# Gated projection weights and the residual's bias of all four batches: made by GpSimd at the start of the attention block instead of by VectorE in the block before

## The reference

```
mod = (silu(c) @ wmod).reshape(B, 6, 1, 256)       # sa, ca, ga, sb, cb, gb
ga  = sign(ga) * max(|ga|, 0.25)
h   = layernorm(x) * (1 + ca) + sa
x   = x + ga * (attention(h) @ W_O + b_O)          # 8 heads, low-rank q, k, v
h   = layernorm(x) * (1 + cb) + sb
x   = x + gb * experts(h)                          # top-1 routing, capacity 768
```

## Time and profile before

| | before |
|---|---|
| time of three runs | 975.48, 975.59, 976.31 us |
| profiled execution: its own time | 975.42 us |
| profiled execution: span | 973.7 us |
| TensorE busy | 865.9 us (89%) |
| VectorE busy | 670.3 us (69%) |
| GpSimd busy | 607.0 us (62%) |
| ScalarE busy | 563.6 us (58%) |

### The profile page before, as it was taken

The page is one execution under the profiler, slowest core; times in us unless marked ns, Lnnn a source line. Parts: engine busy times, 40 slices in busy tenths (PEclk is TensorE's granted clock), DMA queues, the critical chain, the costliest instruction groups (busy, mean ns, idle before and its releaser), DMA issues. The chain is left out here.

```text
span 973.7 us, 20139 instructions
## 1 busy us (share of the span) xinstructions
PE 865.9 (89%) x7974; PEld 605.8 (62%) x7974; DVE 670.3 (69%) x1266; ACT 563.6 (58%) x968; POOL 607.0 (62%) x438
## 2 busy tenths in 40 slices
PE   4895899999999999999999979860799999999995
PEld 1351366666666666666666758760476777677764
DVE  4767887878887878887888609843276567565743
ACT  3641476767676767676767745653447545644650
POOL 5200388888888888888888974786324533452342
PEclk9995699999999999999999989965799999999998
DMA  9911000000000000000000014378434534353110
GB/s 276 335 68 33 1 1 2 3 2 2 2 1 2 2 2 3 2 2 2 2 2 3 2 51 162 120 260 277 145 107 135 183 101 162 129 172 103 43 52 20
DMA packets 52368, 72.32 MB, mean 74 GB/s; under 512 B 11618, under 2 KB 44583, under 8 KB 52048
## 3 DMA queue, kind: packets, MB, share of 16 engines
q1 hardware_dynamic: 42322, 53.93, 16.8%
q0 software_dynamic: 7680, 16.87, 5.3%
q10 hardware_dynamic: 2272, 0.24, 0.2%
HBM read 46.76 MB, written 29.67 MB: 78 GB/s over the span
## 5 line engine op out<-in xcount | busy, mean ns | idle before, releaser
L809 POOL TENSOR_TENSOR prob_lo<-prob 128x1024 f16<-128x1024 f32 x208 | 390.4, 1896 | 120.4 <-ACT prob L781 119.9
L833 DVE TENSOR_REDUCE part_max<-x_ps 128x1 f32<-128x512 f32 x512 | 325.2, 681 | 79.0 <-PE x_ps L730 75.7
L781 ACT ACTIVATE prob<-st_ps 128x512 f32<-128x512 f32 x512 | 281.6, 595 | 114.4 <-PE st_ps L718 108.6
L730 PE MATMUL x_ps<-KX,CQ 98*128 98x512 f16 x512 | 205.0, 405 | 4.0 <-DVE KX L845 1.4
L718 PE MATMUL st_ps<-CQ,KX 99*128 99x512 f16 x512 | 197.2, 386 | 2.8 <-ACT prob L781 1.5
L1304 POOL DMA_INDIRECT out<-yo,xb x48 | 47.7, 994 | 153.4 <-DVE yo L1411 148.5
L756 PE MATMUL acc_ps<-VV,prob 128*128 128x65 f16 x1664 | 128.5, 193 | 2.9 <-POOL prob_lo L809 2.9
L756 PE MATMUL acc_ps<-VV,prob_lo 128*128 128x65 f16 x1664 | 128.1, 193 | 0.0
L756 PEld LDWEIGHTS acc_ps<-VV,prob 128*128 128x128 bf16 x1664 | 116.2, 98 | 18.0 <-DVE both L852 5.0
L756 PEld LDWEIGHTS acc_ps<-VV,prob_lo 128*128 128x128 f16 x1664 | 108.6, 97 | 21.5
L1334 ACT ACTIVATE act_f<-g_ps,cols 128x768 f32<-128x768 f32 x64 | 57.7, 901 | 104.4 <-PE g_ps L1457 103.0
(11 more groups left out here) (172 smaller groups left out, 1256.7 us busy)
## 6 DMA issues: line engine op xcount, KB each, us to landing
w1f<-in_L_ffn_w SPq DMA_DIRECT2D x8, 1024.0 KB, 5.0
w2f<-in_L_ffn_w SPq DMA_DIRECT2D x8, 1024.0 KB
xbuf<-zeros SPq DMA_DIRECT2D x7, 910.0 KB, 17.2
xb<-xbuf SPq DMA_DIRECT2D x8, 780.0 KB
x<-in_L_attn_h_t SPq DMA_DIRECT2D x8, 512.0 KB, 9.0
out<-x SPq DMA_DIRECT2D x4, 1024.0 KB
tbuf<-x SPq DMA_DIRECT2D x4, 1024.0 KB
tbuf<-gb_row SPq DMA_DIRECT2D x4, 1024.0 KB
```

The costliest lines, as they stand in the source:

```text
L730: mm(x_ps[i % 3][:], queries_of[:, n % 2, b * P:(b + 1) * P, j], KX[0:QROWS, n % KRING, f * HALF:(f + 1) * HALF], start=True, stop=True).t ...
L781: nc.scalar.activation(prob[:, k, f * HALF:(f + 1) * HALF], st_ps[i % 2][:], ACT.Exp).then_inc(exp_done, 1)
L809: nc.gpsimd.tensor_tensor(prob_lo[:, k, :], prob[:, k, :], prob_top[:, k, :], ALU.subtract).then_inc(sub_pool, 1)
L833: nc.vector.tensor_reduce(part_max[:, n % 2, j, f:f + 1], x_ps[((n * ST + j) * 2 + f) % 3][:], AX.X, ALU.max).then_inc(smax_done, 1)
```

## The change

The three instructions of `prepare` leave VectorE's list in the first block. The same three are issued by GpSimd, for b = 0 to 3 one after the other, at the head of its list in the second block, ahead of its first `subtract`. The waits for `mod_in`, `side_done` and `ln_xn` are gone with the move; the waits of the instructions on each other are kept. At the end of its second block GpSimd waits for the last of them. `gbias` moves from the memory of the first block to that which is kept through the second.

```diff
@@ memory kept through the second block
+        gbias = sb(inner, "gbias", [P, D])
         mz = sb(inner, "mz", [P, 2, ST], fp16)
@@ memory of the first block
-        gbias = sb(one, "gbias", [P, D])
@@
+        def prepare(pool, b):
+            nc.gpsimd.tensor_tensor(projb[:, b, :, :], proj[:],
+                                    mod[:, b, GA, :].unsqueeze(1).broadcast_to([P, KD, D]), ALU.mult).then_inc(scaled, 1)
+            if b:
+                pool.wait_ge(biased, b)
+            nc.gpsimd.tensor_tensor(gbias[:], attn_bias[:], mod[:, b, GA, :], ALU.mult).then_inc(gbias_done, 1)
+            pool.wait_ge(gbias_done, b + 1)
+            nc.gpsimd.tensor_tensor(x1[:, b * ST:(b + 1) * ST, :], x1[:, b * ST:(b + 1) * ST, :],
+                                    gbias[:].unsqueeze(1).broadcast_to([P, ST, D]), ALU.add).then_inc(biased, 1)
@@ first block, VectorE (the function prepare of L442 to L454 goes)
                 keys_low(2)
-                prepare(0)
                 queries_low(2)
                 side_out(FOLD)
                 side_out(FOLD + 1)
                 take_values(2)
-                prepare(1)
                 keys_low(3)
-                prepare(2)
                 queries_low(3)
                 take_values(3)
-                prepare(3)
@@ second block, GpSimd
+                for b in range(B):
+                    prepare(pool, b)
                 for p, k in slots():
@@
                 normalise(HEADS - 1)
+                pool.wait_ge(biased, B)
```

More of the change, by code:

```diff
@@ L440, in take_values @@
                                             ALU.add).then_inc(v_done, 1)
[L442 to L454, removed]
                 v.wait_ge(turned_rows, 1)
```

## The result

The changed kernel takes 971.67 us, the median of six runs (970.03 to 972.17), against 975.83 us for the kernel before in the same comparison: 4.16 us less, a ratio of 0.9955 with a 95% interval of 0.9942 to 0.9967. The forecast was 970.2 us in a range of 967.8 to 972.9, with 76% on 969.0 to 971.4: the measured median lies in the range, 0.3 us outside that narrower band. The profiled execution took 971.64 us (span 969.9), 3.78 us under that of before (975.42).

The account below looks back on a forecast made before the run. VectorE was taken to bound the kernel only at the first block's end; 2.09 and 3.26 us made 5.35, GpSimd's work cost nothing, so 975.42 - 5.35 = 970.07 us, as a median 970.2, range 967.8 to 972.9.

Parts of the forecast that it names:

- VectorE alone ends the block: End of first block: the boundary waits for VectorE only, which would end at 77.31 instead of 82.66 us, 5.35 us earlier.
- Its two terms: At the boundary: 2.09 us from `queries_low(3)` released by ScalarE instead of VectorE's queue, 3.26 us from `prepare(3)` gone.
- The other 8.3 us: First block: of 13.6 us taken off VectorE, this part lay beside the wait for TensorE and ScalarE and gains nothing.
- GpSimd's twelve instructions: Start of attention: 24.1 us plus 0.8 us of waits, ending at 102.5 us, 1.9 us ahead of the first `subtract`.
- the line through two rows: GpSimd price from below, through L809 and L816: 1.66 ns an element and 0.19 us fixed, 21.0 us for four batches.
- L816's whole ratio: GpSimd price from above: 2.41 ns an element, 6.80 us a batch, 27.2 us in all.
- Cover behind the release: Start of attention: TensorE wants the first `subtract` 3.80 us after its end, so GpSimd may end that much later without loss.
- rival 2: GpSimd as the bound at attention's start: 972.7 us in mild form (6%), 981.2 us in slow form (3%).
- No disturbance between GpSimd and VectorE: Start of attention: VectorE's maxima keep their time beside GpSimd (683 and 681 ns before); GpSimd is priced by L816.
- Everything behind the boundary moves as a whole: From attention to the kernel's end: all comes 5.35 us earlier, since the boundary alone releases attention.
- Rival 1: Start of attention: TensorE's shorter pause keeps the clock from falling, 2.4 us more gained, 967.8 us; 8%.
- Rival 3: Attention or third block: other clock phases or something unseen take the gain back, 975.6 us if all; 7% in full or mostly.

Follow-up runs that it names:

- last_only: Against the changed kernel: only batch 3's three instructions go to GpSimd, those of batches 0 to 2 stay on VectorE; 972.52 us, ratio 0.9969 to before.
- first_three: Against the changed kernel: only batches 0 to 2 go to GpSimd, batch 3 stays at the end of VectorE's list; 973.91 us, ratio 0.9982 to before.
- more_2: The changed kernel with two unneeded products of `projb`'s size added behind the twelve instructions on GpSimd; 971.85 us, ratio 0.9945 to before.
- more_6: The changed kernel with six unneeded products of `projb`'s size added behind the twelve instructions on GpSimd; 980.12 us, ratio 1.0042 to before.
- early_pool: Against the changed kernel: GpSimd does batches 0 to 2 already in its first block, only batch 3 in the second; 973.98 us, ratio 0.9984 to before.
- warm: The changed kernel with twelve tiny VectorE instructions in the old places and unneeded TensorE products in its pause and at attention's start; 966.65 us, ratio 0.9898 to before.
- warm_before: The kernel before, twelve instructions still on VectorE, with unneeded TensorE products in its pause (34) and at attention's start; 972.91 us, ratio 0.9972.

## Why the prediction was right, step by step

- **VectorE alone ends the block; 5.35 us at the boundary.** Right. Measured 5.18, with `keys_low(2)` already 0.18 us later than before (59.28 to 59.46), ahead of every instruction of the change: 5.36 us of its own. Its two terms were measured apart: 3.26 as 3.26 and 2.09 as 2.10 us, counted from `keys_low(2)`.
- **The other 8.3 us, beside the wait for TensorE and ScalarE, are worth nothing.** Right: 8.0 us of idle time appear in front of the three `low` steps, and `last_only` and `first_three` give at the boundary what the list says.
- **GpSimd's twelve instructions: 21.0 to 27.2 us, 24.1 taken, and 0.8 us for waits.** The size was off, not the mechanism. `projb` took 1.26, `gbias` 0.72, x1 4.50 us, and from 77.79 to 103.84 it is 26.05 us with the waits, against 24.9. The four x1 additions have a median of 4506 ns, between the 3.60 us that the line through two rows gave and the 4.9 us of L816's whole ratio. The forecast margin of 1.9 us ahead of the first `subtract` shrank to 0.39.
- **Cover behind the release, 3.8 us more.** Right in kind: `more_2` makes the `subtract` 2.0 us late and loses nothing. In the changed kernel the cover is 3.3 us (the first `subtract` ends at 106.13, the first L748 starts at 109.47). The price beyond it, given in rival 2 as one for one, was too low by more than half: `more_6` loses 8.4 us when the first L748 comes 3.9 us later.
- **No disturbance between GpSimd and VectorE.** Right at this place: VectorE's maxima keep 683 ns (22 of them between 84 and 100 us) beside GpSimd's additions. No row of before showed that it is VectorE's reading of PSUM that keeps the two apart; that was the author's estimate. One block earlier the step would have been wrong: in `early_pool` a cast from SBUF to SBUF took 2.89 instead of 0.37 us, while a TENSOR_SCALAR that reads PSUM kept its 0.57 us.
- **Everything behind the boundary moves as a whole.** This is the step that did not hold, and the median lies 1.4 us above the forecast. In the profiled pair the start of attention gained 0.83 us, attention lost 0.83 again (0.72 of it in two new pauses), the third block's first quarter took 0.83 and what follows 0.57. Only the pauses are tied to the change by an experiment. The start of attention and the first quarter go with the clock's moments, which the forecast carried as ±1.2 us.
- **Rival 1, the clock does not fall.** It fell as the forecast had it, within 77 to 78 us (granted 0.60 in that window, 0.50 behind it). The price of 2.4 us was too low: the profiles show 3.0 us in `warm` and 3.4 in `warm_before`.
- **Rival 3, given back.** It was put down as all or nothing. Between a fifth and a third of the 5.35 us went (4.16 were left between the medians, 3.78 in the profiled pair), in part by what this rival named, a longer stretch at granted 0.50 in the third block (4.8 instead of 3.1 us).
- **The range.** Its upper end of 972.9 us came from GpSimd as the bound, which did not happen. That the measured 971.67 us lies under it is in part luck: the pauses were not thought of.

## What to carry to other kernels

Follow the list of the engine that ends a block backwards and ask of each step who would release it if the step in front were gone; of 13.6 us of removed work only 5.4 counted, and the last 3.4 us of the list gave most of them. Before moving vector work to GpSimd, check two things: until when the consumer of GpSimd's next result can wait, and whether VectorE has casts from SBUF to SBUF or operations on two SBUF tensors beside it, since in `early_pool` a cast took 2.89 instead of 0.37 us and a subtraction 4.76 instead of 0.57 us, ending 0.2 to 0.4 us after GpSimd's addition. Where TensorE pauses for several microseconds, look for a slow clock behind the pause (here granted 0.50 from 78 to 114 us, behind a pause of 8.26 us, and from 78 to 87 us behind one of 3.31 us); unneeded products in the pause and between the first products of attention gained 2.8 us on the kernel before, and `warm` at 966.65 us is faster than both kernels. And before two profiles are compared at a mark, subtract what they differ by ahead of the first changed instruction: with that, the terms of the boundary came out to 0.01 us.

## What the runs showed of the hardware that was not expected

- A VectorE cast from SBUF to SBUF (128x392) took 2.89 instead of 0.37 us, and a subtraction of two SBUF tensors 4.76 instead of 0.57 us, while GpSimd's addition of 128x2048 ran; they ended 0.2 and 0.4 us after it. A row maximum that reads SBUF (128x16, at 95.18 us in the changed kernel) kept its 0.17 us beside GpSimd's work. The subtraction has two inputs in SBUF, the cast one; what held them up is not shown.
- Taking twelve instructions out of VectorE's first block brought two pauses of 0.26 us at 198 and 434 us, and each cost 0.36 us; twelve instructions on one column in their places took them away.
- A wait of TensorE of 4.1 us was followed by 11 us at granted 0.50 in which TensorE was busy nearly all the time (2.00 of each 2 us from 114 to 124), and the run lost 8.4 us in all.
